# Cross-attention on one core: the first batch's key and query projections cut into column halves

## The reference

```python
q = einsum('bcn,dc->bnd', x1, Wq) + bq
k = einsum('bcn,dc->bdn', x2, Wk) + bk[:, None]
v = einsum('bcn,dc->bdn', x2, Wv) + bv[:, None]
attn = softmax(einsum('bnd,bdm->bnm', q, k), axis=2)
out = einsum('bcm,bnm->bcn', v, attn) + x1
```

## Time and profile before

| | |
|---|---|
| median of 3 runs | 645.95 us (645.71 to 646.01) |
| the profiled execution | 646.25 us, of it a span of 644.5 us from first to last instruction |
| TensorE busy (matmul) | 637.9 us |
| VectorE, ScalarE, GpSimd busy | 460.8, 344.9, 113.7 us |
| moved by DMA | 100.11 MB, 155 GB/s in the mean |

### The profile page before, as it was taken

How to read it: one execution, slowest core, us unless ns; L and a number is a source line. 1 busy time by engine, 2 the same in 40 slices (tenths; PEclk the granted TensorE clock), 3 DMA queues, 4 the chain that set the end, 5 groups by cost and what they waited for, 6 DMA issues and landing times.

```text
span 644.5 us, 9671 instructions
## 1 busy us (share of the span) xinstructions
PE 637.9 (99%) x3489; PEld 520.9 (81%) x3489; DVE 460.8 (71%) x523; ACT 344.9 (54%) x446; POOL 113.7 (18%) x50
## 2 busy tenths in 40 slices
PE   8999999999999999999999999999999999999997
PEld 5878888888888888888888888888888888888886
DVE  5897749857598476984778946789558885598441
ACT  5887636735467344574454753555626647276120
POOL 0012200332005300063000620006200152002100
PEclk9999999999999999999999999999999999999999
DMA  8903445962259722677327763287532973434442
GB/s 307 358 3 70 117 125 145 306 150 95 90 156 314 173 79 94 162 277 179 96 67 201 255 163 98 65 229 255 135 119 72 243 240 107 130 93 119 111 122 94
DMA packets 40495, 100.11 MB, mean 155 GB/s; under 512 B 7328, under 2 KB 7584, under 8 KB 40480
## 3 DMA queue, kind: packets, MB, share of 16 engines
q1 hardware_dynamic: 40480, 99.91, 51.6%
HBM read 51.64 MB, written 16.78 MB: 106 GB/s over the span
## 4 chain that ended last, share of the span: by engine, by line
PE 93%; ACT 2%; DVE 2%; DMA 1%; SPq 1%; issue 0%; DVEq 0%
PE acc_ps L994 44%; PE acc_ps L972 15%; PE acc_ps L1010 9%; PE acc_ps L962 9%; PE s_ps L912 8%; PE s_ps L928 6%; DMA stage<-in_x_dram 1%; DVE pt_lo L607 1%; PE s_ps L920 1%; PE s_ps L921 0%; DVE negmax L674 0%; ACT k_hh L358 0%; SPq L293 0%; ACT pt_hi L358 0%; ACT vt_hi L358 0%
## 5 line engine op out<-in xcount | busy, mean ns | idle before, releaser
L994 PE MATMUL acc_ps<-pt_hi,vt_hi 128*128 128x512 f32 x421 | 163.9, 389 | 0.0
L994 PE MATMUL acc_ps<-pt_lo,vt_hi 128*128 128x512 f32 x421 | 163.8, 389 | 0.0
L994 PE MATMUL acc_ps<-pt_hi,vt_lo 128*128 128x512 f32 x421 | 163.8, 389 | 0.0
L322 POOL TENSOR_TENSOR pt_lo<-pt_raw,pt_hi 128x1024 fp32r<-128x1024 f32 x14 | 39.6, 2829 | 361.3 <-ACT pt_hi L358 361.3
L994 PEld LDWEIGHTS acc_ps<-pt_hi,vt_hi 128*128 128x128 f32 x421 | 79.0, 188 | 16.7 <-DVE pt_lo L607 0.3
L994 PEld LDWEIGHTS acc_ps<-pt_hi,vt_lo 128*128 128x128 f32 x421 | 79.0, 188 | 16.5
L994 PEld LDWEIGHTS acc_ps<-pt_lo,vt_hi 128*128 128x128 f32 x421 | 79.0, 188 | 16.3
L322 POOL TENSOR_TENSOR xs_lo<-stage,xs_hi 128x1024 fp32r<-128x1024 f32 x29 | 71.9, 2502 | 107.4 <-ACT xs_hi L358 107.4
L674 DVE TENSOR_REDUCE negmax<-s_ps 128x1 f32<-128x1024 f32 x64 | 77.6, 1213 | 17.8 <-PE s_ps L930 15.6
L450 ACT ACTIVATE probs<-s_ps,negmax 128x1024 f32<-128x1024 f32 x56 | 62.6, 1117 | 44.7 <-DVE negmax L674 43.8
L358 ACT ACTIVATE pt_hi<-pt_raw 128x1024 fp32r<-128x1024 f32 x60 | 62.0, 1057 | 27.2 <-PE acc_ps L994 26.6
(11 more groups left out here) (133 smaller groups left out, 1368.2 us busy)
## 6 DMA issues: line engine op xcount, KB each, us to landing
pt_raw<-blocks SPq DMA_DIRECT2D x240, 128.0 KB, 2.4
stage<-in_x_dram SPq DMA_DIRECT2D x32, 512.0 KB, 6.3
o_sb<-in_x_dram SPq DMA_DIRECT2D x64, 256.0 KB, 3.4
out_dram<-o_sb SPq DMA_DIRECT2D x64, 256.0 KB, 2.5
stage<-in_ctx_dram SPq DMA_DIRECT2D x31, 512.0 KB, 8.9
pt_raw<-in_L_xattn_Wv_dram SPq DMA_DIRECT2D x4, 256.0 KB, 6.9
stage<-in_ctx_dram SPq DMA_DIRECT2D x2, 256.0 KB, 3.2
pt_raw<-in_L_xattn_Wk_dram SPq DMA_DIRECT2D x1, 128.0 KB, 2.9
```

The lines of the kernel that those rows point to most:

```text
L322: return nc.gpsimd.tensor_tensor(out, src, hi.bitcast(F32), ALU.subtract)
L994: mm = nc.tensor.matmul(acc_ps[:, c % BANKS, :], v[:, m, cols], p[:, m, :], start=(m == 0 and v is vt_hi and p is pt_hi), stop=(m == MT - ...
```

## The change

It concerns the first batch, and in `move` all batches.

- SP loads x2 tile 1 in two column halves as well (heads 0 and 1 first, each followed by its Wv tile, then Wk, then both tails). Wq comes before x1 tile 0. The 16 DMAs of `move` are issued in another order.
- The key projection is done for columns 0 to 511 and 512 to 1023 apart, and so are cross copy, sum, high part, its copy, low part and its copy.
- The query's first half goes to slot 1 of `s_ps`, the second into accumulator bank 3 (`Q_BANK`), projected after scores(0) and scores(1). x1 tiles 1 to 3 are split in halves.
- TensorE, ScalarE and VectorE have a new order in the prologue; scores(5) stands ahead of the outputs.
- Outputs of half 0 of the first batch go to other accumulator banks, and the waits of half 1 are fitted to that.

```diff
+Q_BANK = 3
+        def out_bank(h, c, first):
+            return (c + 2) % BANKS if first and h == 0 else c % BANKS
...
@@ SP, move @@
-                for i in range(NQ):
-                    for j in range(NQ):
+                for step in range(NQ):
+                    for i in range(NQ):
+                        j = (i + step) % NQ
...
@@ SP, first loads @@
+            for k in range(HEADS):
+                head(k)
+                weight(k)
             sp.dma_start(wk_raw, wk_d.rearrange("p (k d) -> p k d", d=D)).then_inc(s_wk, 16)
+            for k in range(HEADS):
+                tail(k)
+            for k in range(HEADS, KT):
                 load_x2(0, k)
                 weight(k)
+            sp.dma_start(wq_raw, wq_d.rearrange("p (k d) -> p k d", d=D)).then_inc(s_wq, 16)
             load_x1(0, 0)
...
@@ ScalarE, first batch, from x1 tile 0 on @@
+            first_x1_hi(0)
+            first_k_cross_a()
             first_x1_hi(1)
             first_v_hi(0)
+            first_x1_hi_a(2)
             first_k_high(0)
             first_v_hi(1)
+            first_x1_hi_a(3)
+            first_k_high_copy(0)
+            first_k_cross_b()
+            first_v_hi(2)
+            first_k_low_copy(0)
+            first_q_cross_a()
             first_k_high(1)
+            first_k_high_copy(1)
             first_q_high_a()
+            first_v_hi(3)
+            first_k_low_copy(1)
+            first_x1_hi_b(2)
+            first_x1_hi_b(3)
             first_v_hi(4)
             first_exp(0)
+            first_q_cross_b()
             first_exp(1)
             first_v_hi(5)
             first_normalise(1)
             first_p_hi(0)
             first_exp(2)
             first_exp(3)
+            first_q_high_b()
...
@@ VectorE, first batch, from x1 tile 0 on @@
+            first_x1_lo(0)
+            first_k_sum_a()
+            first_x1_lo_a(1)
             first_v_lo(0)
+            first_x1_lo_a(2)
+            first_k_low(0)
+            first_x1_lo_a(3)
             first_v_lo(1)
+            first_k_sum_b()
+            first_x1_lo_b(1)
+            first_q_sum_a()
+            first_k_low(1)
+            first_v_lo(2)
             first_q_low_a()
+            first_v_lo(3)
+            first_x1_lo_b(2)
+            neg_max(0, 0)
+            first_x1_lo_b(3)
+            neg_max(0, 1)
+            first_normalise(0)
+            first_q_sum_b()
             first_v_lo(4)
             inverse(1)
             neg_max(0, 2)
             first_v_lo(5)
...
@@ VectorE, outputs of half 0 (order unchanged) @@
+            def out(b, h, c, first=False):
-                    out=o_sb[:, c, :], in0=acc_ps[:, c % BANKS, :], scalar=bias_v[:, c:c + 1],
+                    out=o_sb[:, c, :], in0=acc_ps[:, out_bank(h, c, first), :], scalar=bias_v[:, c:c + 1],
...
@@ TensorE @@
+            def out_part(b, h, c, m, first=False):
+                if m == 0 and first and h == 1 and c < 2:
+                    pe.wait_ge(s_acc, BANKS + MT + 2 + c + 1)
+                elif m == 0:
                     pe.wait_ge(s_acc, b * ACC + MT + h * CT + c + (2 if (h, c) == (0, 0) else 1))
...
-                        if first and (c, m) == (0, 1):
-                            scores(5)
-                        if first and (c, m) == (0, 3):
+                        if first and (c, m) == (0, 4):
                             scores_next(0, 6)
...
@@ first_turn(0) @@
-                    pe.wait_ge(s_acc, BANKS + 5)
+                    pe.wait_ge(s_acc, BANKS + 4)
+                    pe.wait_ge(s_qsum, 1)
...
@@ TensorE, first batch, behind value tile 0 @@
             first_k(0, 0)
+            pe.wait_ge(s_headlo, 2)
+            first_k(1, 0)
+            pe.wait_ge(s_wvhi, 2)
+            first_v_term(1, xs_hi, wv_hi)
             pe.wait_ge(s_x2lo_e, 1)
             first_k(0, 1)
+            first_v_term(1, xs_lo, wv_hi)
+            pe.wait_ge(s_x2lo_o, 1)
+            first_k(1, 1)
+            pe.wait_ge(s_wvlo, 2)
+            first_v_term(1, xs_hi, wv_lo)
+            pe.wait_ge(s_x2lo_e, 2)
+            first_k(2, 0)
+            pe.wait_ge(s_wvhi, 3)
+            first_v_term(2, xs_hi, wv_hi)
+            pe.wait_ge(s_wvlo, 3)
+            first_v_term(2, xs_hi, wv_lo)
             pe.wait_ge(s_x2lo_o, 2)
+            first_k(3, 0)
+            first_v_term(2, xs_lo, wv_hi)
             pe.wait_ge(s_wvlo, KT)
+            first_v_last(0)
+            first_v_last(1)
             pe.wait_ge(s_wqlo, 1)
+            pe.wait_ge(s_x1lo_e, 1)
+            first_q_a(0)
+            first_v_last(2)
+            first_q_a(1)
+            first_k(2, 1)
+            first_k(3, 1)
+            first_v_last(3)
+            first_q_a(2)
+            first_q_a(3)
             first_v_group(4)
             first_v_group(5, part=0)
+            pe.wait_ge(s_kcopy, 4)
             pe.wait_ge(s_qlo_a, 1)
             scores(0)
+            pe.wait_ge(s_acc, BANKS + 4)
+            first_q_b(0)
+            pe.wait_ge(s_qsum_a, 1)
             scores(1)
+            first_q_b(1)
+            first_q_b(2)
+            first_q_b(3)
             first_v_group(5, part=1)
             scores_next(0, 2)
             pe.wait_ge(s_ident, 1)
             first_turn(0)
             scores_next(0, 3)
+            first_v_group(6)
             first_turn(1)
             first_turn(2)
             first_turn(3)
+            first_v_group(7)
             pe.wait_ge(s_qlo, 1)
             pe.wait_ge(s_plo, 2)
             scores(4)
             pe.wait_ge(s_plo_odd, 2)
+            scores(5)
             batch(0, False, first=True)
```

More of the change, by code:

```diff
@@ L54 @@
 OUTS = 4
+HEADS = 2
 Q = 32
@@ L136, in build @@
         s_warm = sem("s_warm")
-        s_head = sem("s_head")
+        s_head = [sem(f"s_head_{k}") for k in range(HEADS)]
         s_headhi = sem("s_headhi")
         s_headlo = sem("s_headlo")
+        s_xhi_a = sem("s_xhi_a")
+        s_xlo_a = sem("s_xlo_a")
+        s_ka = sem("s_ka")
+        s_kcross_a = sem("s_kcross_a")
+        s_ksum_a = sem("s_ksum_a")
+        s_kcopy = sem("s_kcopy")
         s_qa = sem("s_qa")
@@ L787, in batch @@
                     low_x1(nb, 3)
-                out(b, 0, 0)
-                out(b, 0, 1)
+                out(b, 0, 0, first)
+                out(b, 0, 1, first)
                 if not last:
@@ L798, in batch @@
                     q_low(nb)
-                out(b, 0, 2)
-                out(b, 0, 3)
+                out(b, 0, 2, first)
+                out(b, 0, 3, first)
                 out(b, 1, 0)
@@ L848, in _, with first_x1_lo_b @@
+            def first_x1_lo_b(k):
+                dve.wait_ge(s_x1hi, k + 1)
+                sub(x0_lo[:, k, NH:N], stage1[:, k, NH:N], x0_hi[:, k, NH:N]).then_inc((s_x1lo_e, s_x1lo_o)[k % 2], 1)
             nc.vector.memset(probs[:, 0, 0:NH], 0.0).then_inc(s_warm, 1)
             nc.vector.memset(negmax[:], 0.0).then_inc(s_acc, BANKS)
-            dve.wait_ge(s_headhi, 1)
-            sub(xs_lo[:, 0, 0:NH], stage2[:, 0, 0:NH], xs_hi[:, 0, 0:NH]).then_inc(s_headlo, 1)
-            weight_lo(0)
+            for k in range(HEADS):
+                head_lo(k)
+                weight_lo(k)
@@ L993, in out_part @@
                 for v, p in ((vt_hi, pt_hi), (vt_hi, pt_lo), (vt_lo, pt_hi)):
-                    mm = nc.tensor.matmul(acc_ps[:, c % BANKS, :], v[:, m, cols], p[:, m, :],
+                    mm = nc.tensor.matmul(acc_ps[:, out_bank(h, c, first), :], v[:, m, cols], p[:, m, :],
                                           start=(m == 0 and v is vt_hi and p is pt_hi),
@@ L1047, in batch @@
                             q_next(nb)
-                        out_part(b, 0, c, m)
+                        out_part(b, 0, c, m, first)
                 for c in range(CT):
@@ L1065, in batch @@
                         else:
-                            out_part(b, 1, c, m)
+                            out_part(b, 1, c, m, first)
                 if last:
@@ L1107, in first_turn, with first_k @@
                 mm.then_inc(s_blk, 1)
-            def first_k(k, part):
-                for h in range(HALVES):
-                    mm = nc.tensor.matmul(s_ps[:, 0, h, :], wk_s[:, k, :],
-                                          (xs_hi, xs_lo)[part][:, k, h * NH:(h + 1) * NH],
+            def first_k(k, h):
+                for part, x in enumerate((xs_hi, xs_lo)):
+                    mm = nc.tensor.matmul(s_ps[:, 0, h, :], wk_s[:, k, :], x[:, k, h * NH:(h + 1) * NH],
                                           start=(k == 0 and part == 0), stop=(k == KT - 1 and part == 1))
-                return mm
+                if k == KT - 1:
+                    mm.then_inc((s_ka, s_k)[h], 1)
             def first_v_term(k, x, w):
@@ L1137, in first_v_group, with first_q, first_q_a, first_q_b @@
                     mm.then_inc(s_v, 1)
-            def first_q(k):
-                pe.wait_ge((s_x1lo_e, s_x1lo_o)[k % 2], k // 2 + 1)
-                for h in range(HALVES):
```

(22 more changed lines are left out.)

204 lines of the change are left out of this document (99 added, 105 removed).

## The result

The changed kernel takes 653.22 us (652.60 to 653.48, five runs) against 646.01 for the kernel before in the same comparison, a ratio of 1.011 with a 95% interval of 1.0096 to 1.0125. The forecast was 652.0 us in a range of 649.4 to 653.8.

What follows compares the result with a forecast made beforehand. TensorE was taken to bound the kernel, without a gap after the first batch's early waits. 646.25 - 1.8 (prologue) + 5.9 (bank-swap stall) + 2.0 (fallen clock) = 652.35, lowered 0.3 for the median to 652.0 us; range 649.4 to 653.8.

Steps and rivals of the forecast that it cites:

- The bank swap: At the first batch's half 1 start, TensorE waits for VectorE's third output addition: 5.9 us lost, bounds 5.5 to 6.3.
- The clock: After that 5.9 us pause TensorE falls to 1.2 GHz for a while: about 2.0 us lost, bounds 0 to 4.
- The prologue: First batch's start: 2.7 us of old TensorE idling goes, 0.9 new comes, so 1.8 us won; bounds +2.7 and -0.5.
- The beginning: TensorE's first matmuls start at 5.03 us, with 0.41 us extra for their slow beginning.
- Wk: TensorE's first 32 matmuls, value and key tiles 0 and 1, run without a wait and end at 12.70 us.
- x2 tile 2: Before first_k(2, 0), TensorE waits for this tile's low part until 13.2 us: 0.6 us with the restart.
- scores(0): First scores start at 26.5 us; their inputs are done at 25.9, so covered by 0.6 us.
- The moves: 16 block moves in rotated order in every half batch: 1.3 us of slack, so cost taken as 0.
- the thinly covered turns: First batch: first_turn(0) covered by only 0.2 us; first_turn(1) waits 0.1 us, plus 0.1 for the restart.
- That the clock stays high: Rival: same stall at half 1 but no slow stretch behind it, 650.0 us; chance 0.27.
- The faster one: Rival: VectorE reaches the third output addition before TensorE ends half 0, no stall, 644.2 us; chance 0.04.

Runs made afterwards that it cites:

- the filling: Changed kernel with 24 more matmuls of 512 columns, results overwritten, put where TensorE pauses before half 1: 650.91 us, ratio 1.0075.
- the unswapped kernel: Changed kernel with half 0's outputs back in bank c, and waits for the low parts of value rows 6 and 7 instead: 644.82 us, on another chip 644.98.
- the trial with the earlier additions: Changed kernel, swap kept, first batch's third output addition moved ahead of VectorE's four low parts and the fourth right behind them: 644.79 us, ratio 0.9983.

## Why the prediction was right, and where its terms were off

**The bank swap (5.9 us predicted).** Right in place, releaser, chain and size: 5.80 measured, where the 5.9 has a restart of 0.1 that the 1.45 us below contain. It is shown as the cause from both sides, by adding it alone to the kernel before and by taking it away from the changed one. The reason that it could be sized so closely is that every piece of the loop stood in the old trace, only without TensorE waiting at its end.

**The clock (2.0 us).** Right that it falls. The size is 1.45 in the profiled execution, the fastest of the five, 2.50 in the trace of the swap alone, and 2.2 to 2.3 by the medians with and without the filling. It differs between executions, with how long the slow level lasts. The 2.0 was taken from one slow stretch at the start of the old trace (half of its 4.4 us is 2.2, rounded down); it fits the size, but with prices between 1.45 and 2.50 that it lies among them is partly luck. The argument for the fall, that 5.9 us is six times the pause that kept the clock, asked for more than was needed: 2.6 us are enough in three of six runs.

**The prologue (1.8 us won).** This is the term that was mis-sized. The profiled execution of the changed kernel has 0.86, and the unswapped kernel is 1.0 to 1.1 us under the kernel before in the median. By the prediction's sum scores(0) starts at 26.5; it starts at 27.52. Four steps of that sum were off.

- *The beginning, 0.3 us.* The prediction kept the old start, 5.03, and the old excess of the slow beginning, 0.41. The first twelve matmuls start at 5.14 and have an excess of 0.64 over their usual 2.72 us.
- *Wk, 0.7 us.* The prediction has TensorE's first 32 matmuls follow each other, without a wait for the second x2 head or for Wk, which now comes behind that head and its Wv tile. The head came late, ScalarE took it up at 6.69 and Wk at 7.87 (below), and Wk's low part held TensorE until 9.08: 0.58 us and the restart.
- *x2 tile 2, 0.6 us the other way.* The wait that was expected there did not come: the tile was early (ScalarE takes it up at 10.26), its low part was ready at 12.58, and TensorE asks at 13.79.
- *scores(0), 0.6 us.* It was thought covered by 0.6 us, its copies done at 25.9. They are done at 27.47, and TensorE would have been there at 26.94. From the first key cross copy on, at 16.71, the profile lists no wait of ScalarE. Its last ten instructions up to there, from 21.07 to 27.47, take 0.64 us each from start to start, where the ones of the same size just before them stand about 0.5 apart; the prediction had "about 0.6 us for a half". They don't wait for VectorE: the second key sum ends at 23.15 and is used at 24.25, the query sum at 25.10 and 25.56, the key's low part at 25.81 and 26.84. So ScalarE's list is what holds scores(0); why its instructions stand 0.64 apart there isn't shown.

Together 0.3 + 0.7 - 0.6 + 0.6 gives the 1.0 us by which scores(0) is late. ScalarE's timeline at the late head:

```profile
6.69 0.63 ACT L378 ACTIVATE xs_hi<-stage 128x512 fp32r<-128x512 f32 x1 [1.69 <-DMA stage<-in_ctx_dram]
7.33 0.63 ACT L378 ACTIVATE wv_hi<-pt_raw 128x512 fp32r<-128x512 f32 x1
7.87 0.40 ACT L378 ACTIVATE wk_s<-pt_raw 128x256 fp32r<-128x256 f32 x1
```

In the unswapped kernel's first trace the second head was there at 5.29 and no wait for Wk appears; half 1 starts at 71.89, 1.66 before. This is near the predicted 1.8 partly by luck, since the missing wait at x2 tile 2 and the wait before scores(0) cancel. It also compares an execution 0.3 us below its median (644.53) with one 0.3 above (646.25 for the kernel before); the medians give 1.1. The arrival of that head varies, 5.2 to 6.7 us in the seven traces with this load order, and the changed kernel's profiled one is the latest. The slow beginning varies too. The second trace of the unswapped kernel has no wait for Wk either, and yet half 1 starts at 72.51, because its first matmuls are slow for longer:

```profile
4.97 2.05 PE L1214 MATMUL acc_ps<-wv_hi,xs_hi 128*128 128x512 f32 x4
6.82 1.49 PE L1214 MATMUL acc_ps<-wv_hi,xs_lo 128*128 128x512 f32 x4
8.14 1.09 PE L1214 MATMUL acc_ps<-wv_lo,xs_hi 128*128 128x512 f32 x4
```

against 5.10, 6.59 and 7.51 for the same starts in the first. So the prologue's gain is between 0.9 and 1.7 us by single traces, and both mis-sized terms, this one and the clock, put the forecast under the measured time.

**The moves (0)** and **the thinly covered turns**: right. first_turn(0) did not wait; first_turn(1) started 0.15 us late, where 0.1 was laid out.

**The rivals.** That the clock stays high is refuted by the granted clock of 0.50 and by the filled pause, which gives 650.9 where this rival had 650.0; most of the difference is the prologue's gain of 1.1 instead of 1.8 us. The faster one is refuted as the change stands, but the trial with the earlier additions shows that its condition was the right one: once VectorE reaches the third addition in time, the kernel takes 644.8, near that rival's 644.2.

## What to carry to other kernels

When a buffer is given to another user, look at what stands in the list ahead of the instruction that frees it, and whether any of it waits for the engine that will ask. Here it cost 5.8 us in each of the three traces that have it, wherever TensorE's half 0 ended. On an engine that is otherwise never idle, add the clock to the price of a pause; here 5.8 us of waiting cost 8.1. Splitting work into halves to start sooner puts more instructions into the lists of the other engines; here ScalarE's list then held scores(0) and kept 0.6 us of the gain.

## What was unexpected of the hardware

- A pause of 2.56 us brought TensorE's clock down in three of six executions of the same program, by their times and mean clocks, at a price of 1.8 us; the pause of about 1 us in the kernel before did so in none of the three traces that have it (the kernel before, with the swap, with the rotated moves).
- The same pause of 5.8 us cost 1.45 us of slow matmuls in one trace and 2.50 in another.
- 24 useless matmuls in the pause saved 2.2 to 2.3 us: keeping the engine at work was worth more than leaving it idle.
- The second half-tile load of x2 (256 KB, third in SP's queue and issued at 1.66 us) was taken up by ScalarE at 5.16 to 6.69 us in the seven traces with the same load order.
- How long the first matmuls stay slow differs between executions of one program: the twelve of value tile 0 take 3.34 us in one trace of the unswapped kernel and 4.09 in the other.
